# Moving the last batch's GroupNorm and convolutions to earlier slots in a fused channel-mixing and deformable-convolution kernel

## The reference, cut to what matters

```python
x = x + mix(groupnorm(x), W0, b0)            # mix: per batch, xn = g / |g| over channels
                                             # s = relu(xn^T xn)^2 (1024 x 1024), y = (W0 g + b0) s
x = x + relu(deform(groupnorm(x), offset))   # offset = conv3x3(conv3x3(groupnorm(x), w1, b1), w2, b2), 72 channels
```

## Time and profile before

| | |
|---|---|
| median of the runs | 460.2 us (459.57 to 460.83) |
| profiled execution | 459.05 us, of which the span from first to last instruction is 457.0 us |
| TensorE busy | 405.2 us (89%) |
| VectorE busy | 339.5 us (74%) |
| ScalarE busy | 215.6 us (47%) |
| GpSimd busy | 90.0 us (20%) |
| TensorE's mean granted clock | 0.97 |
| the chain that ended last | TensorE 46%, VectorE 32%, DMA 6%, SyncE's queue 5% |

### The profile page before, as it was taken

The page is one execution under the profiler, slowest core; times in us unless marked ns, Lnnn a source line. Parts: engine busy times, 40 slices in busy tenths (PEclk is TensorE's granted clock), DMA queues, the critical chain, the costliest instruction groups (busy, mean ns, idle before and its releaser), DMA issues.

```text
span 457.0 us, 9689 instructions
## 1 busy us (share of the span) xinstructions
PE 405.2 (89%) x3887; PEld 291.9 (64%) x3887; DVE 339.5 (74%) x586; ACT 215.6 (47%) x392; POOL 90.0 (20%) x99
## 2 busy tenths in 40 slices
PE   6698989979998789799999798989869898979996
PEld 6455557646665565678666575768556566857875
DVE  5995776829999999388854999376979945779901
ACT  3343254345555365441655446331845643257661
POOL 5444470001774100000546100000010000000000
PEclk9899999999999899999999899989979997999999
DMA  7200002250011124332001313442213243303330
GB/s 252 77 0 0 0 2 75 84 141 1 2 47 46 47 67 146 85 90 91 12 13 36 92 54 94 124 126 81 59 47 100 90 122 98 104 23 107 96 105 24
DMA packets 46157, 32.71 MB, mean 72 GB/s; under 512 B 3264, under 2 KB 43488, under 8 KB 46112
## 3 DMA queue, kind: packets, MB, share of 16 engines
q1 hardware_dynamic: 46048, 31.95, 23.5%
q10 hardware_dynamic: 64, 0.13, 0.1%
HBM read 25.24 MB, written 10.37 MB: 78 GB/s over the span
## 4 chain that ended last, share of the span: by engine, by line
PE 46%; DVE 32%; DMA 6%; SPq 5%; issue 4%; ACT 4%; POOL 1%; DVEq 0%; ACTq 0%; POOLq 0%
PE psB L788 10%; PE psB L555 9%; PE psT L739 7%; DVE wpix L1507 7%; PE psV L762 5%; DVE combo L1294 4%; PE psA L646 4%; DMA h_scr<-h_ring 3%; SPq L320 3%; DVE combo_p L1298 2%; DVE tent L1488 2%; PE psA L555 2%; DVE tent L1482 2%; PE psB L813 2%; PE psA L813 2%
## 5 line engine op out<-in xcount | busy, mean ns | idle before, releaser
L1021 ACT ACTIVATE wcell<-psT 128x512 f32<-128x512 f32 (+1 forms) x160 | 83.9, 552 | 70.2 <-PE psT L739 68.9
L1507 DVE TENSOR_TENSOR wpix<-tent 128x512 f32<-128x512 f32 (+1 forms) x160 | 99.7, 675 | 14.4 <-PE psT L739 13.3
L739 PE MATMUL psT<-ident,wpix 128*128 128x128 f32 x576 | 89.1, 288 | 12.4 <-ACT wcell L1021 12.0
L739 PEld LDWEIGHTS psT<-ident,wpix 128*128 128x128 f32 x576 | 68.8, 148 | 37.2 <-issue 29.5
L493 POOL TENSOR_TENSOR sim<-rel 128x512 f32<-128x512 f32 x48 | 61.4, 1299 | 69.0 <-ACT rel L978 69.0
L1045 ACT ACTIVATE val<-psV 128x576 f32<-128x576 f32 x64 | 44.0, 688 | 30.7 <-PE psV L762 30.2
L788 PE MATMUL psB<-val,wd_sb 128*128 128x256 f32 x216 | 51.2, 392 | 0.0
L762 PE MATMUL psV<-wcell,hwin 64*32 64x144 f32 x2048 | 47.2, 294 | 3.9 <-ACT val L1045 3.5
L646 PE MATMUL psA<-sim,scratch 128*128 128x512 f32 x96 | 45.6, 597 | 0.6 <-POOL sim L493 0.6
L788 PEld LDWEIGHTS psB<-val,wd_sb 128*128 128x128 f32 x216 | 40.7, 193 | 8.3 <-issue 2.9
L555 PE MATMUL psB<-g_p 128*128 128x512 f32 x144 | 40.9, 419 | 0.0
(11 more groups left out here) (193 smaller groups left out, 453.6 us busy)
## 6 DMA issues: line engine op xcount, KB each, us to landing
hwin<-h_scr SPq DMA_DIRECT2D x128, 128.0 KB, 2.9
h_scr<-h_ring SPq DMA_DIRECT2D x8, 576.0 KB
h_ring<-sim SPq DMA_DIRECT2D x4, 512.0 KB
x_all<-x SPq DMA_DIRECT2D x1, 1536.0 KB, 10.0
out<-yout SPq DMA_DIRECT2D x12, 128.0 KB, 1.8
off_scr<-sim SPq DMA_DIRECT2D x4, 288.0 KB
combo<-sim SPq DMA_DIRECT2D x32, 32.0 KB
val<-w SPq DMA_DIRECT2D x1, 576.0 KB, 6.1
```

Of the source, the lines that this page charges most:

```text
L739: last = pe.transpose(bank[:, at:at + P], wpix[:, t % 2, k, 2 * h:2 * h + 2, :].rearrange("p g q -> p (g q)"), ident[:, :])
L1021: act.activation(wcell[:, t % 2, taps[0]:taps[-1] + 1, :, :].rearrange("q k h p -> q (k h p)"), bank[:, 0:len(taps) * G // 2 * P], ACT.Cop ...
L1507: dve.tensor_tensor(w, ty, tx, ALU.mult).then_inc(s["weights_done"], 1)
```

## The change: the last batch's front in other slots

- The fourth batch's group mean and variance go into the tail of the second batch (into `psA`): the mean behind the first quarter's contraction, the variance between the second quarter's sixth tap and the tail's last sample. On VectorE `spread` follows the first output addition, normalisation and the first two combinations stand ahead of the last. On ScalarE the square root and two high copies come ahead of the last ReLU.
- In the third batch the first convolution takes the slots 4 to 17, the image is turned in 21, the second convolution takes 25 to 40, and the offsets are turned in 56 and 58. Weights for tile t stand in the slots of tile t-2 in which TensorE turns, the first weights of the fourth batch in 60 instead of 67.
- SyncE stores and lays the image and shifts the offsets one tile earlier, the shifts ahead of the windows of tile 6.
- The extremes of the last batch move from slot 70 of the third batch to slot 18 of the fourth, `turn_farthest` to slot 24, the flag to slot 38.
- The slots of all fronts are now lists. For the lead-in and the first two batches the lists hold the old slots. VectorE's loop over v issues, for each v, its combination if it has this slot and then its subtraction if it has this slot.

```diff
+        def moments_at(b):
+            return psA[:, 1, 0:2] if b == B - 1 else psB[:, 0, 0:2]
...
+        def in_a_row(combine, high, conv):
+            return dict(combine=[range(n, n + V) for n in combine], low=[range(n + 1, n + 1 + V) for n in combine],
+                        high=[range(n, n + V) for n in high], conv=[range(n, n + 3 * V // 2) for n in conv],
+                        copy=[n + 3 for n in conv], sums=[n + 4 for n in conv], rows=[n + 5 for n in conv])
...
+        STEADY = dict(in_a_row((29, 43), (30, 44), (36, 49)), mean=23, dev=24, var=25, norm=28, flat=28, image=33, wrap=55,
                       shift=None, turn={65: (0, 1), 67: (2, 3)}, extremes=70)
+        SPREAD_OUT = dict(combine=[(-1, -1, 3, 5), (19, 20, 23, 25)], low=[(0, 1, 5, 7), (21, 22, 25, 27)],
+                          high=[(-1, -1, 4, 6), (20, 21, 24, 26)], conv=[(4, 7, 8, 13, 16, 17), (25, 26, 31, 34, 35, 40)],
+                          copy=[9, 32], sums=[17, 36], rows=[18, 41], mean=None, dev=None, var=None, norm=None, flat=2,
+                          image=21, wrap=42, shift=None, turn={56: (0, 1), 58: (2, 3)}, extremes=None)
...
+        W_EVEN = {t: tuple(K * (t - 2) + k for k in TURN_SLOT) for t in range(2, ROWT)}
+        LEAD_WEIGHTS, FIRST_WEIGHTS, LAST_WEIGHTS, LEAD_EXTREMES = 60, 67, 60, 12
+        LAST_EXTREMES, LAST_FARTHEST, LAST_FLAG = 18, 24, 38
...
# SyncE
+                    image, lay, shifts = (4, 5, 6) if b + 1 == LAST else (5, 6, 7)
...
# TensorE: tail
                 dconv(b, 0, nxt, prep, range(6, K))
+                if b + 2 == LAST:
+                    group_mean(LAST, 0)
                 sample(b, ROWT - 1, 0)
                 dconv(b, 1, nxt, prep, range(6))
+                if b + 2 == LAST:
+                    group_mean(LAST, 1)
                 sample(b, ROWT - 1, 1)
...
# ScalarE: tail
+                if b + 2 == LAST:
+                    std(LAST)
                 take_samples(b, ROWT - 1, 1)
+                for m in range(1, 3):
                     relu_out(b, m)
+                if b + 2 == LAST:
+                    conv_front(LAST, -1, SPREAD_OUT)
+                relu_out(b, 3)
...
# VectorE: front loop
                 for which in range(2):
-                    if 0 <= n - at["combine"][which] < V:
-                        combine_rows(b, which, n - at["combine"][which])
-                    if 0 < n - at["combine"][which] <= V:
-                        split_rows(b, which, n - at["combine"][which] - 1)
+                    for v in range(V):
+                        if n == at["combine"][which][v]:
+                            combine_rows(b, which, v)
+                        if n == at["low"][which][v]:
+                            split_rows(b, which, v)
...
# VectorE: fourth batch, and tail
+                        if b == LAST and n == LAST_EXTREMES:
+                            find_extremes(LAST)
+                            find_farthest()
+                        if b == LAST and n == LAST_FLAG:
+                            set_flag()
...
                 add_out(b, 0)
+                if b + 2 == LAST:
+                    spread(LAST)
+                for i in range(len(TAPS)):
+                    weights(nxt, 1, i)
+                for m in range(1, 3):
                     add_out(b, m)
+                if b + 2 == LAST:
+                    normalise_x1(LAST)
+                    conv_front(LAST, -1, SPREAD_OUT)
+                add_out(b, 3)
```

More of the change, by code:

```diff
@@ L526, in batch_steps @@
                             square(b + 2, SCORE.index(n))
-                        if nxt is not None and n == STEADY["wrap"]:
+                        if nxt is not None and n == front(nxt)["wrap"]:
                             wrap_offsets(nxt)
-                        if nxt is not None and n == STEADY_FLAT:
+                        if nxt is not None and n == front(nxt)["flat"]:
                             copy_flat(nxt)
@@ L659, in conv @@
                         pe.wait_ge(s["combo_lo"], n)
-                    if kx == 0 and which == 0 and v == 2:
+                    if kx == 0 and v == 2 and which == (1 if b == LAST else 0):
                         pe.wait_ge(s["image_copied"], 2 * (b + 1))
@@ L865, in batch_steps @@
                         n = K * t + k
+                        if b == LAST and n == LAST_FARTHEST:
+                            turn_farthest()
                         if k in TURN_SLOT:
@@ L881, in batch_steps @@
                                 prepare(prep, what)
-                        if nxt is not None and n == STEADY_IMAGE:
+                        if nxt is not None and n == front(nxt)["image"]:
                             turn_image(nxt)
                         if nxt is not None:
-                            conv_front(nxt, n, STEADY, prep)
+                            conv_front(nxt, n, front(nxt), prep)
                 if b == LAST:
@@ L1096, in batch_steps @@
                         if nxt is not None:
-                            conv_front(nxt, n, STEADY)
-                        if nxt is not None and n == STEADY_IMAGE + 1:
+                            conv_front(nxt, n, front(nxt))
+                        if nxt is not None and n == front(nxt)["image"] + 1:
                             copy_image(nxt)
@@ L1620, in batch_steps @@
                         if nxt is not None:
-                            conv_front(nxt, n, STEADY)
-                        for tile, slots in W_AT.items():
+                            conv_front(nxt, n, front(nxt))
+                        if b == LAST and n == LAST_EXTREMES:
[3 more added lines that the diff above has]
+                            set_flag()
+                        for tile, slots in (W_EVEN if nxt == LAST else W_AT).items():
                             for i in range(len(TAPS)):
@@ L1625, in batch_steps @@
                                     weights(b, tile, i)
-                        if nxt is not None and n == FIRST_WEIGHTS:
+                        if nxt is not None and n == (LAST_WEIGHTS if nxt == LAST else FIRST_WEIGHTS):
                             for i in range(len(TAPS)):
@@ L1633, in batch_steps @@
                 add_out(b, 0)
-                if nxt is not None:
-                    for i in range(len(TAPS)):
-                        weights(nxt, 1, i)
-                for m in range(1, 4):
+                if b + 2 == LAST:
[3 more added lines that the diff above has]
+                for m in range(1, 3):
                     add_out(b, m)
+                if b + 2 == LAST:
+                    normalise_x1(LAST)
+                    conv_front(LAST, -1, SPREAD_OUT)
+                add_out(b, 3)
             dve.nop().then_inc(s["yout_done"], YOUT0)
```

62 lines of the change are left out of this document (30 added, 32 removed).

## The result

The changed kernel takes 476.1 us (median of 4 runs, 475.2 to 479.2) against 460.3 for the kernel before beside it: a ratio of 1.0356, interval 1.0308 to 1.0404. The profiled execution took 475.24 us, with a span of 473.3. The forecast was 474.8 us, from 464 to 482.

What follows compares the result with a forecast made beforehand. Nothing saturated; the order in which engines wait for each other sets the time. Terms 1.5 + 6.2 + 2.0 - 1.8 + 3.3 + 3.4 = +14.6 us, on the median 460.2, gave 474.8 us, range 464 to 482.

Steps and rivals of the forecast that it cites:

- Order in the slot: First two batches: VectorE subtracts before combining and waits for ScalarE's copy, 3.1 us each, 6.2 together.
- 3.4 of clock: New waits in the early batches and tail: two clock falls counted at 1.7 us each.
- bound of 8.5 for five falls: Upper bound of the clock term, if the clock falls at all five new waits; as a rival, chance 0.15.
- Lead: Before the first batch: the same order delays the last combination, 0.7 to 2.0 us, taken as 1.5.
- Tail: Second batch's tail: TensorE waits for the variance ahead of the last sample; 2.0 us with the matmuls.
- Third batch: 81.5 us against 83.3, -1.8; waits of 3 us at slot 24 and 4.8 at slot 56.
- the step that named the shifts as its only cause: Third batch, slot 56: TensorE waits 4.8 us for shifted offsets, their transposes moved further than the transfer.
- Fourth batch: Start wait gone, -1.4; farthest offset holds TensorE 2.9 us longer at slot 24, clock 2.2, window -0.4: +3.3.
- The free order: Rival, order within a slot: ScalarE's copy is always in time, 463.7 us; chance 0.12.
- The evenly packed batch: Rival, third batch: neither slot 24 nor 56 waits, batch takes 68 us, time 461.3; chance 0.10.
- the shared transfers: Rival, third batch: shifts share the transfers' engines and land later, 6.4 us more, 481.2; chance 0.08.

Runs made afterwards that it cites:

- both flips: Old order within a slot put back in the changed kernel, 464.4 us; new order alone put into the kernel before, 477.5 us.
- order_back: Changed kernel with VectorE again combining before it subtracts in a slot that holds both: 464.4 us, ratio 1.0108.
- turn_late: Changed kernel with the third batch's transposes of the shifted offsets back at slots 65 and 67: 475.3 us, ratio 1.0313.
- lay_last: Changed kernel with the third batch's image layout transfer behind the shifts (tile 7), not ahead of tile 5's windows: 478.95 us, ratio 1.0429.
- all_lay_halves: All mends, with the layout transfer on SyncE in two halves, ahead of the windows of tiles 5 and 7: 454.7 us, ratio 0.9873.
- turn_and_lay: Changed kernel with offsets' transposes at 65 and 67 and the layout transfer between tile 5's windows and the shifts: 480.0 us, ratio 1.0413.
- the other mends: On the changed kernel: old order, combinations at slot 18, offsets' transposes at 65/67, farthest 32, flag 44, later variance matmul; 455.2 us with GpSimd's layout transfer.
- after: The changed kernel itself, in its profiled execution: 475.24 us, median of the runs 476.1 us.
- all_mended: Changed kernel with old order, combinations at 18, offsets' transposes at 65/67, layout transfer behind tile 5's windows, farthest 32, flag 44, later variance matmul: 461.5 us.
- lay_pool: Changed kernel with the third batch's layout transfers issued by GpSimd at its slot 30 instead of SyncE: 475.8 us, ratio 1.0336.

## Why the prediction was right, and where its terms were off

*Order in the slot.* Right in place and sign, shown by both flips. Mis-sized between its parts: it counted 6.2 us of stalls, and 3.4 of clock with the tail's, 9.6 together, where 10.6 were measured up to the second batch's offsets. But the idle time of TensorE grew by only 1.8 and 2.4 us there, and its busy time, for the same 974 and 732 instructions, by 5.3 and 1.1 (the tail has 1.6 and 0.6 more). So the stalls were about 4.2 and the clock about 6.4, nearly twice its term and toward the bound of 8.5 for five falls. That one was too large by 2 and the other too small by 3 is why the sum is so near: that is luck. Nor is all of it the order's: `order_back` gives back 8.9 of the 10.6, and 1.6 are the fall after a wait that was there before. The prediction took that wait's 1.00 in the earlier trace rows as evidence against falls; in the changed kernel and in `order_back` the same wait is followed by 0.72 and 0.56.

*Lead.* 1.5 forecast, 1.95 measured, and 3.0 given back by `order_back`: five of the lead's eight subtractions stood 0.72 or 0.73 us for their copy, one 0.41, one 3.35 and one not at all.

*Tail.* 2.0 forecast, 2.18 measured: TensorE waits 1.24 us for the variance, not 1.7, and VectorE's three operations end at 324.78. That this wait alone sets the tail was not tried by itself.

*Third batch.* 81.5 forecast, 80.85 measured, with the wait at slot 24 as worked out (3.0; 3.10) and that at the end near its size (4.8; 5.78 and 0.45). The shifted offsets came 54.5 us after the batch's start where 53.5 were said, and what followed took 26.4 where the forecast had 28.0; these two errors cancel in part. But the step that named the shifts as its only cause failed: the windows of tile 5 were late as well, at the same time, by the layout transfer ahead of them. The prediction weighed a late landing for the shifts; it did not for the windows, though the earlier trace rows had one of 9.3 us. `turn_late` and `lay_last` show that either lateness alone is enough: taking away one leaves 5.74 us for the other, or 4.26.

*Fourth batch.* +3.3 forecast, +2.7 measured: 3.40 us for the farthest where 2.9 longer than ScalarE's 0.39 was said, and the clock at 0.67 for 4.5 us behind it, 1.5 us and not 2.2.

*The rivals.* The free order is refuted. The evenly packed batch did not come: even in `all_lay_halves`, the fastest kernel here, the third batch takes 77.4 us where that rival had 68. Of the shared transfers little is shown at the shifts: from the first shift's issue to the first transposed offset it took 9.9 us (379.54 to 389.43) where the layout transfer was ahead, and 8.0 in `lay_last` (379.08 to 387.03), where it was behind; 1.9 us of the 6.4 that were the bound. And 1.6 of these are SyncE's issue (7.71 us against 6.13), which takes 6.06 in `turn_and_lay`, right behind the transfer; what slows it in the change stays open. It was at the windows that the transfer told. The Trainium skill, "DMA: Bandwidth & Descriptors", section "Issuing engines are not separate DMA queues", says that transfers run on the same 16 engines whichever engine issues them; the one trace of `lay_pool` agrees, with a window of SyncE's at 9.4 us beside the transfer from GpSimd.

*The load's 1.33 us* belongs to no step: of the 16.3 us between the two executions the forecast's own steps made 15.0, where they said 14.6.

## What to carry to other kernels

A loop that is only rewritten can change the order within a step: list each engine's instructions before and after, and ask of each pair that changed places what its wait was covered by. When two things that one engine needs at one point are late together, removing one shows nothing; look at when each lands, not at the wait that is named. A large transfer can be moved only to where what follows it has slack, or be cut into parts with other work between. Moving it to another engine's queue alone did not help (475.8 us against 476.1); with the other mends, moving it there, and so to an earlier point, did (455.2 against 461.5).

## What the runs showed of the hardware that was not expected

The slowest of the four windows issued next behind or beside the 1.15 MB layout transfer landed 8.8, 9.7, 9.3 and 9.4 us after its issue (`after`, `turn_and_lay`, `all_mended`, `lay_pool`), for the tiles 5, 6, 6 and 4, and in the last case with the transfer on GpSimd's queue; the median window takes 2.9. In `lay_last` TensorE began the sample of tile 7 9.5 us after the last of its windows was issued.

The clock does not follow the length of the wait. After 1.38 us (271.86) it is 0.61 from 272 to 279 us; after the same releaser's 2.65 us it is 0.74 at 183.6 to 187 and 1.00 at 296.1 to 299.5:

```profile
183.60:187.00 3.40, 3.40 (x41) 2.02 (x42) 3.30 (x7) 1.43 (x3) 0.00 (x0) 0.74 0.30 117
...
296.10:299.50 3.40, 3.39 (x44) 2.09 (x45) 3.30 (x7) 2.10 (x4) 0.00 (x0) 1.00 0.29 111
```

Nor does it follow the place: after the wait of 2.68 or 2.69 us that three kernels share in their first batch it stayed at 1.00 in the kernel before and was 0.72 and 0.56 in `after` and `order_back`. So a forecast of single falls from one execution is a guess; in the first two batches their sum was nearer to the prediction's bound for five than to its two.
